# ScalarE normalises all four input tiles, VectorE joins the fourth, and GpSimd makes the factors before its last residual tile

## Chip, cores and metric

The kernel runs on one core of a Trainium2 chip. The metric is the device time of one launch in microseconds; the median of three runs is given.

## The reference, cut to what matters

The input x is (2, 4096, 512) in float32. Two blocks follow one another, each adding to its input.

```python
s  = sigmoid(silu(x @ s_w1.T + s_b1) @ s_w2.T + s_b2)      # x: layernorm of the input
u  = (x @ B_w.T + B_b) * s
h  = h @ A.T + u_t                                        # step by step over 4096 rows
y  = hs @ C_w.T + C_b + x @ D_w.T + D_b
x1 = input + y * sigmoid(x @ g_w.T + g_b)

chosen = argmax(layernorm(x1) @ gate_w.T)                 # one of 8 experts a row
out    = x1 + layernorm(x1) @ expert_w[chosen].T
```

The change touches only the first layernorm of x, the turning of its rows into columns, and the moment at which x1's last quarter is made.

## The kernel before, in words

The 8192 rows go through 16 bodies (b = 0 to 15) of 512 rows: two sequences, 256 rows of each, in four tiles of 128 rows (NT = 4). A body is written out by hand for each engine, as one long list, and the engines meet at semaphores. Every matmul has float32 operands split in a high and a low part, so one product is three matmuls (L1476 to L1478, `mm3`). After the bodies come 71 slots that apply the experts to sorted rows; the change leaves them alone.

What stands in body b on TensorE (L1638): `y_state(b-1)` (four products with the state of the body before), the two `s1` products of all four tiles, the `scan` product, then y and gate products of the four tiles with the steps of the scan strewn in between: `to_pairs`, `to_chunks`, `over(0)` to `over(5)`, `to_middles`, `down`. Each step of the scan is a small matmul (L1620 or L1476), VectorE's sum of its result (L1050, L1052 or L1058), and VectorE's split into high and low: a CAST (L1042) and a subtraction (L1044) that read and write SBUF. The next step on TensorE waits for the split. The first gate product of tile i waits for `gate_sum(b, i-1)` (L1080), which empties the bank.

The input of body b+1 is made during body b, tile by tile:
- SyncE loads it to `xin`; VectorE makes statistics and mean and variance (`ln1_stats`, `ln1_mv`, L992 and L998).
- GpSimd makes the factors `rs1` and `shift1` for four tiles at once (`rstd1`, L573).
- Tiles 0 and 1 are normalised by ScalarE (L756), tiles 2 and 3 by GpSimd (`normalise_late`, L632), which stands behind `rstd1`, the scatter and `add_identity`.
- ScalarE copies the float32 rows as two planes of 16 bits (`halve`, L768), SyncE turns them with a DMA transpose (`flip`, L370), ScalarE joins the planes again (`join`, L795) and makes the high part (`high`, L802), VectorE the low part (`low`, L1249). The first s1 product of the next body needs all four high parts, its last four matmuls (L1665) all four low parts.

GpSimd's list in body b (L635): `residual(b-1)` for four tiles, each two multiplications (L592) and two additions (L596) of 128x256; `rstd1(b+1)`; `scatter(b-2)`, four indirect DMAs (L618); `add_identity` (L627); `normalise_late` twice; `rstd2(b-1)` (L602 and on), which waits for VectorE's `ln2_mv` (L1097). The residual tiles make x1. Tiles 2 and 3 of x1 are turned by DMA as well in bodies 2 to 14: ScalarE `halve_x1` (L731), SyncE (L458), ScalarE `join_x1` (L737).

VectorE's list ends with `h_lo` (L1354, waits for ScalarE's copy L892), `low(b+1, 1)`, `place` (L1132 to L1141), `low_piece` (L1242, expert weights), `low(b+1, 2)`, `ln2_mv`, `gate_sum(b, 3)`; the next body starts with `low(b, 3)` and `y_biased`.

SyncE issues its transposes in the order x1 tile 2, x1 tile 3, input tiles 0, 1, and later 2, 3.

Of the kernel before, what the change touches and what calls it, by code (L numbers as in the profile page):

```python
# [5 lines left out]
def preln_ssm_moe_kernel(nc, x, A, B_w, B_b, C_w, C_b, D_w, D_b, s_w1, s_b1, s_w2, s_b2, g_w, g_b,  # L6
# [27 lines left out]
    NT = TB // P  # L34
# [40 lines left out]
    with ExitStack() as keep:  # L75
# [109 lines left out]
        for name in ("first_half_loaded bias_loaded cols_loaded A_loaded s1_loaded aux_loaded xin_loaded consts_made consts2_made pad_made ident_made "  # L185
                     "bias_sum w_turned w_hi w_lo pow_psum pow_copied pow_hi pow_lo "
                     "gate_stats gate_mean gate_centred stats1 mv1_ready ve1_ready rstd1_ready neg1_ready shift1_ready xn_ready xn_late xT_psum x_halves joined xT_hi xT_lo "
# [168 lines left out]
        def _(sp):  # L356
# [73 lines left out]
            for b in range(NBLK):  # L430
# [24 lines left out]
                if by_dma(b - 1, NT - 1):  # L455
                    for j in range(2):
                        sp.wait_ge(S_["x1_halves"], 2 * (b - 2) + j + 1)
                        sp.dma_start_transpose(x1_flipped[j], x1_halves[j]).then_inc(x1_turned[j], 16)  # L458
                for n in range(NB):
                    if not last:  # L460
                        flip(b + 1, 2 * n)
                        flip(b + 1, 2 * n + 1)
                    if b + 2 < NBLK:
                        load_x(b + 2, n)
                    if n == 0 and b > 1:
                        load_residual(b, b % 2, b // 2)
# [81 lines left out]
        def _(pool):  # L548
# [24 lines left out]
            def rstd1(b):  # L573
                counted_waits(pool, (S_["mv1_ready"], b + 1))
                nc.gpsimd.tensor_scalar(ve1[:], mv1[:, :, 1], EPS, None, ALU.add).then_inc(S_["ve1_ready"], 1)
                pool.wait_ge(S_["ve1_ready"], b + 1)
                if b > 0:
                    pool.wait_ge(S_["xn_ready"], NT + NT // 2 * (b - 1))
                    wait(pool, S_["xn_late"], NT // 2 * (b - 1))
                nc.gpsimd.tensor_tensor(rs1[:], ve1[:], mhalf[:], ALU.pow).then_inc(S_["rstd1_ready"], 1)  # L580
                counted_waits(pool, (S_["shift1_ready"], b))
                nc.gpsimd.tensor_scalar(neg1[:], mv1[:, :, 0], -1.0, None, ALU.mult).then_inc(S_["neg1_ready"], 1)
                counted_waits(pool, (S_["neg1_ready"], b + 1), (S_["rstd1_ready"], b + 1))
                nc.gpsimd.tensor_tensor(shift1[:], neg1[:], rs1[:], ALU.mult).then_inc(S_["shift1_ready"], 1)

            def residual(b, q):
                pool.wait_ge(xres_loaded[q], 16 * NB * (b // 2 + 1))
                for i in range(NT):
# [40 lines left out]
            def normalise_late(b, i):  # L629

                pool.wait_ge(S_["shift1_ready"], b + 1)
                nc.gpsimd.tensor_scalar(xin[:, i, :], xin[:, i, :], rs1[:, i:i + 1], shift1[:, i:i + 1],  # L632
                                        ALU.mult, ALU.add).then_inc(S_["xn_late"], 1)

            def body(b, q):  # L635
                if b > 0:
                    residual(b - 1, 1 - q)
                if b < LASTB:
                    rstd1(b + 1)
                if b >= 2:  # L640
# [4 lines left out]
                if b < LASTB:  # L645
                    normalise_late(b + 1, 2)
                    normalise_late(b + 1, 3)
# [43 lines left out]
        def _(act):  # L691
# [67 lines left out]
            def halve(b, i):  # L759

                n = turn_of(b, i)
                if i < NT // 2:
                    normalise1(b, i)
                    act.wait_ge(S_["xn_ready"], NT + NT // 2 * (b - 1) + i + 1)
                else:
                    act.wait_ge(S_["xn_late"], NT // 2 * (b - 2) + i + 1)
# [38 lines left out]
            def body(b):  # L805
# [42 lines left out]
                if dma:  # L848
                    halve_x1(b - 1, 2)
                    halve_x1(b - 1, 3)  # L850
                if ahead:
                    halve(b + 1, 0)
# [40 lines left out]
                if ahead:  # L893
# [3 lines left out]
                    join(b + 1, 3)  # L897
# [88 lines left out]
        def _(dve):  # L986
# [265 lines left out]

            def body(b, q, turn):
# [104 lines left out]
                if tail:  # L1358
                    place(old, oldq, oldturn)
                    if dma:  # L1360
# [515 lines left out]
```

## Time and profile before

| | before |
|---|---|
| median of 3 runs | 909.34 us (908.67 to 910.84) |
| profiled execution | 911.03 us |
| its span, first to last instruction | 909.2 us |
| TensorE busy (PE) | 890.7 us, 98% |
| VectorE (DVE) | 684.2 us, 75% |
| ScalarE (ACT) | 635.5 us, 70% |
| GpSimd (POOL) | 426.8 us, 47% |
| granted TensorE clock, mean | 0.998 |

The shares are means over the whole span. Bodies 1 to 15 begin at 56.5, 98.1, 138.8, 179.8, ... and 631.2 us, when `y_state` of the body before begins on TensorE; body 7 begins at 302.73 and body 8 at 343.73. The slots follow the last body. The end of a matmul is modelled in the profile; its start is what can be compared.

### The profile page before, as it was taken

The page shows a single profiled execution, that of the slowest core. Times are in us where ns is not written, and L with a number is a line of the kernel's source. Part 1 is how long each engine was busy: PE and PEld are TensorE (multiplying, and loading weights), DVE is VectorE, ACT ScalarE, POOL GpSimd, SP SyncE. Part 2 cuts the span into 40 slices and gives each one's busy share as a digit, 9 for nine tenths or more (in the row PEclk, how much of TensorE's full clock was granted, in tenths as well). Part 3 has the DMA queues.
Part 4 walks back from the last instruction along what each step waited for, and adds up shares of the span by engine and source line. Part 5 has one row for each costly group of instructions (what it writes and reads, how often), then busy time and mean ns, then how long its engine had stood idle before and what let it go on. Part 6 is the DMA issues. An engine that isn't in the chain of part 4 may idle for free. (4 is left out here: it accounts for less than half of the span.)

```text
span 909.2 us, 15716 instructions
## 1 busy us (share of the span) xinstructions
PE 890.7 (98%) x4413; PEld 719.8 (79%) x4414; DVE 684.2 (75%) x1697; ACT 635.5 (70%) x880; POOL 426.8 (47%) x671
## 2 busy tenths in 40 slices
PE   8999999999999999999999999999999999999996
PEld 7778878787887878787787878787878887888884
DVE  6778888888887888888887888888686465555552
ACT  5568697978879687977879687978634445666661
POOL 1134537282735537282836546282624453433442
PEclk9999999999999999999999999999999999999999
DMA  9436495867758486867768495856989979998871
GB/s 319 131 93 148 93 213 140 200 144 193 157 155 209 101 213 137 201 145 189 148 169 206 95 221 128 202 145 161 293 285 401 370 239 252 216 226 220 196 184 49
DMA packets 231050, 172.37 MB, mean 190 GB/s; under 512 B 155701, under 2 KB 189237, under 8 KB 229952
## 3 DMA queue, kind: packets, MB, share of 16 engines
q1 hardware_dynamic: 220032, 137.71, 60.8%
q0 software_dynamic: 10800, 33.70, 11.3%
q8 instruction: 35, 0.57, 0.3%
q14 instruction: 39, 0.32, 0.1%
q10 hardware_dynamic: 144, 0.07, 0.0%
HBM read 81.63 MB, written 54.68 MB: 150 GB/s over the span
## 5 line engine op out<-in xcount | busy, mean ns | idle before, releaser
L1798 PE MATMUL y<-experts,x1T_hi 128*128 x568 | 180.5, 399 | 0.7 <-DVE x1T_lo L1422 0.7
L666 POOL DMA_INDIRECT out<-gate,ids x71 | 72.6, 1023 | 110.3 <-DVE gate L1441 69.0
L602 POOL TENSOR_SCALAR ln_var_eps<-ln_mean_var 128x4 f32<-128x4 f32 x16 | 3.7, 231 | 252.6 <-DVE ln_mean_var L1097 252.5
L1798 PEld LDWEIGHTS y<-experts,x1T_hi 128*128 128x128 f32 x568 | 103.2, 188 | 20.6 <-issue 0.9
L1798 PE MATMUL y<-experts,x1T_lo 128*128 x284 | 111.4, 392 | 0.0
L1476 PE MATMUL gates<-GwT_hi,xT_hi 128*128 128x512 f32 x256 | 105.0, 410 | 1.6
L592 POOL TENSOR_TENSOR y_biased<-y_biased,gate 128x256 f32<-128x256 f32 x120 | 94.1, 805 | 23.8 <-DVE y_biased L1087 23.6
L1476 PE MATMUL y<-DwT_hi,xT_hi 128*128 128x512 f32 x256 | 102.6, 401 | 0.0
L1441 DVE TENSOR_TENSOR gate<-y,raw_weights 128x512 f32<-128x512 f32 x71 | 49.1, 691 | 69.2 <-PE y L1798 65.1
L1478 PE MATMUL gates<-GwT_hi,xT_lo 128*128 128x512 f32 x256 | 100.6, 393 | 0.0
L1477 PE MATMUL gates<-GwT_lo,xT_hi 128*128 128x512 f32 x256 | 100.6, 393 | 0.0
L1478 PE MATMUL y<-DwT_hi,xT_lo 128*128 128x512 f32 x256 | 100.3, 392 | 0.0
L1477 PE MATMUL y<-DwT_lo,xT_hi 128*128 128x512 f32 x256 | 100.2, 392 | 0.0
L596 POOL TENSOR_TENSOR x_rows<-x_rows,y_biased 128x256 f32<-128x256 f32 x120 | 86.7, 743 | 4.7
L795 ACT ACTIVATE joined<-flipped 128x1024 uint16<-128x1024 uint16 x60 | 81.9, 1366 | 8.5 <-DMA flipped<-halves 6.4
L618 POOL DMA_INDIRECT routed_rows<-x_rows,dest x64 | 64.4, 1006 | 24.2 <-issue 23.4
L909 ACT ACTIVATE x1T_hi<-turned 128x512 fp32r<-128x512 f32 x36 | 21.6, 599 | 68.0 <-PE turned L1787 68.0
L768 ACT ACTIVATE halves<-x_in 128x1024 uint16<-128x1024 uint16 x60 | 63.0, 1050 | 1.0
L1798 PEld LDWEIGHTS y<-experts,x1T_lo 128*128 128x128 f32 x284 | 53.3, 188 | 12.0
L1050 DVE TENSOR_TENSOR z<-scan,z 128x126 f32<-128x126 f32 (+6 forms) x128 | 36.0, 281 | 32.2 <-PE scan L1620 30.6
L1476 PEld LDWEIGHTS gates<-GwT_hi,xT_hi 128*128 128x128 f32 x256 | 48.1, 188 | 12.5 <-DVE gate L1080 4.2
L1478 PEld LDWEIGHTS gates<-GwT_hi,xT_lo 128*128 128x128 f32 x256 | 48.1, 188 | 11.1
(285 smaller groups left out, 2335.1 us busy)
## 6 DMA issues: line engine op xcount, KB each, us to landing
raw_weights<-routed_rows SPq DMA_DIRECT2D x71, 258.0 KB, 3.2
x_in<-L_attn_x SPq DMA_DIRECT2D x32, 512.0 KB, 4.5
x_rows<-L_attn_x SPq DMA_DIRECT2D x32, 512.0 KB, 4.9
turned_experts<-raw_weights SPq DMA_DIRECT2D x32, 512.0 KB, 3.5
experts<-turned_experts SPq DMA_DIRECT2D x8, 2048.0 KB, 14.7
raw_weights<-L_ffn_expert_w SPq DMA_DIRECT2D x32, 256.0 KB, 3.1
routed_rows<-padrow SPq DMA_DIRECT2D x9, 258.0 KB
out<-gate,ids POOLq DMA_INDIRECT x71, 4.1
```

Of the source, the lines that this page charges most:

```text
L592: ins = nc.gpsimd.tensor_tensor(yb[:, i, part], yb[:, i, part], gate[:, i, part], ALU.mult)
L596: ins = nc.gpsimd.tensor_tensor(xrow[q][:, i, part], xrow[q][:, i, part], yb[:, i, part], ALU.add)
L618: nc.gpsimd.indirect_dma_start(out=routed, out_offset=bass.IndirectOffsetOnAxis(ap=dest[q][:, i:i + 1], axis=0), in_=xrow[q][:, i, :], in_ ...
L666: nc.gpsimd.indirect_dma_start(out=out_rows, out_offset=bass.IndirectOffsetOnAxis(ap=ids[r][:, 0:1], axis=0), in_=res[r], in_offset=None, ...
L768: nc.scalar.activation(halves[n % 2][:].rearrange("p (h d) -> p h d", h=2), planes(xin[:, i, :]), ACT.Copy).then_inc(S_["x_halves"], 1)
L795: nc.scalar.activation(planes(joined[n % 2][:].rearrange("p k t -> p (k t)")), flipped[n % 2][:].rearrange("p (h k) t -> p h (k t)", h=2), ...
L1050: nc.vector.tensor_tensor(states, both[:, 0], states, ALU.add).then_inc(S_["scan_part"], 1)
L1441: nc.vector.tensor_tensor(res[r], Y[m % 2][:], rows[m][:, 0:D], ALU.add).then_inc(S_["slot_result"], 1)
L1476: nc.tensor.matmul(dst, left[0], right[0], start=first, stop=False)
L1477: nc.tensor.matmul(dst, left[0], right[1], start=False, stop=False)
L1478: return nc.tensor.matmul(dst, left[1], right[0], start=False, stop=last)
L1798: ins = nc.tensor.matmul(Y[m % 2][:], x2T[a][:, k, m % 2 * P:(m % 2 + 1) * P], flat[:, bass.ds(first + (w * KD + k) * D, D)], start=(k == ...
```

## The change

ScalarE normalises all four tiles of the input in `halve`. VectorE gets a function `join` and does the join of tile 3, between `place` and `low_piece`. GpSimd does `rstd1` between residual tile 2 and residual tile 3, and no normalisation. In bodies 2 to 14 ScalarE's `halve(b+1, 0)` stands between `halve_x1` of tiles 2 and 3, and SyncE's transposes follow in the same order. The semaphore `xn_late` is gone, and the counts on `xn_ready` are adapted.

```diff
@@ sync
                         sp.dma_start_transpose(x1_flipped[j], x1_halves[j]).then_inc(x1_turned[j], 16)
+                        if j == 0:
+                            flip(b + 1, 0)
                 for n in range(NB):
                     if not last:
-                        flip(b + 1, 2 * n)
+                        if n > 0 or not by_dma(b - 1, NT - 1):
+                            flip(b + 1, 2 * n)
                         flip(b + 1, 2 * n + 1)
@@ gpsimd
-                if b > 0:
-                    pool.wait_ge(S_["xn_ready"], NT + NT // 2 * (b - 1))
-                    wait(pool, S_["xn_late"], NT // 2 * (b - 1))
+                wait(pool, S_["xn_ready"], NT * b)
...
-            def normalise_late(b, i):
-
-                pool.wait_ge(S_["shift1_ready"], b + 1)
-                nc.gpsimd.tensor_scalar(xin[:, i, :], xin[:, i, :], rs1[:, i:i + 1], shift1[:, i:i + 1],
-                                        ALU.mult, ALU.add).then_inc(S_["xn_late"], 1)
-
             def body(b, q):
                 if b > 0:
-                    residual(b - 1, 1 - q)
+                    residual(b - 1, 1 - q, range(NT - 1))
                 if b < LASTB:
                     rstd1(b + 1)
+                if b > 0:
+                    residual(b - 1, 1 - q, range(NT - 1, NT))
...
-                if b < LASTB:
-                    normalise_late(b + 1, 2)
-                    normalise_late(b + 1, 3)
@@ scalar
             def halve(b, i):
 
+                normalise1(b, i)
                 n = turn_of(b, i)
-                if i < NT // 2:
-                    normalise1(b, i)
-                    act.wait_ge(S_["xn_ready"], NT + NT // 2 * (b - 1) + i + 1)
-                else:
-                    act.wait_ge(S_["xn_late"], NT // 2 * (b - 2) + i + 1)
+                act.wait_ge(S_["xn_ready"], NT * b + i + 1)
...
                 if dma:
                     halve_x1(b - 1, 2)
+                if ahead:
+                    halve(b + 1, 0)
+                if dma:
                     halve_x1(b - 1, 3)
                 if ahead:
-                    halve(b + 1, 0)
                     halve(b + 1, 1)
...
                     high(b + 1, 2)
-                    join(b + 1, 3)
@@ vector
+            def join(b, i):
+
+                n = turn_of(b, i)
+                dve.wait_ge(x_turned[n % 2], 16 * (n // 2 + 1))
+                dve.wait_ge(S_["joined"], n)
+                dve.wait_ge(S_["xT_lo"], NT + n - 1)
+                nc.vector.tensor_copy(planes(joined[n % 2][:].rearrange("p k t -> p (k t)")),
+                                      flipped[n % 2][:].rearrange("p (h k) t -> p h (k t)", h=2)
+                                      ).then_inc(S_["joined"], 1)
...
                 if tail:
                     place(old, oldq, oldturn)
+                if ahead:
+                    join(b + 1, 3)
+                if tail:
                     if dma:
                         low_piece(b, 0)
```

## Rows read from the trace of the kernel before

**Rows 1.** Timeline of TensorE, body 7: start us, us, engine, line, what.

```profile
328.72 0.39 PE L1478 MATMUL y<-DwT_hi,xT_lo 128*128 128x512 f32 x1
...
330.10 0.39 PE L1477 MATMUL gates<-GwT_lo,xT_hi 128*128 128x512 f32 x1
```

**Rows 2.** Timeline of TensorE, the same place in bodies 2 and 14.

```profile
124.07 0.40 PE L1478 MATMUL y<-DwT_hi,xT_lo 128*128 128x512 f32 x1
...
125.17 0.40 PE L1477 MATMUL gates<-GwT_lo,xT_hi 128*128 128x512 f32 x1
...
616.13 0.39 PE L1478 MATMUL y<-DwT_hi,xT_lo 128*128 128x512 f32 x1
...
617.53 0.39 PE L1477 MATMUL gates<-GwT_lo,xT_hi 128*128 128x512 f32 x1
```

**Rows 3.** Timeline of VectorE, body 7, around the split after `over(1)`.

```profile
327.74 0.68 DVE L1042 CAST chunk_ends<-z 128x124 fp32r<-128x124 f32 x1
328.46 0.65 DVE L1044 TENSOR_TENSOR chunk_ends<-z,chunk_ends 128x124 fp32r<-128x124 f32 x1
329.03 0.68 DVE L1080 TENSOR_TENSOR gate<-gates,g_bias 128x512 f32<-128x512 f32 x1
...
330.33 0.23 DVE L1042 CAST chunk_ends<-z 128x120 fp32r<-128x120 f32 x1
330.59 0.29 DVE L1044 TENSOR_TENSOR chunk_ends<-z,chunk_ends 128x120 fp32r<-128x120 f32 x1
```

**Rows 4.** Timeline of GpSimd, body 7 (in brackets: idle before, and what ended it).

```profile
304.42 0.24 POOL L602 TENSOR_SCALAR ln_var_eps<-ln_mean_var 128x4 f32<-128x4 f32 x1 [16.42 <-DVE ln_mean_var L1097]
...
315.37 1.98 POOL L592 TENSOR_TENSOR y_biased<-y_biased,gate 128x256 f32<-128x256 f32 x2
...
318.94 0.23 POOL L575 TENSOR_SCALAR ln_var_eps<-ln_mean_var 128x4 f32<-128x4 f32 x1
...
321.60 1.09 POOL L618 DMA_INDIRECT routed_rows<-x_rows,dest  x1 [0.62 <-issue]
...
327.38 1.59 POOL L632 TENSOR_SCALAR x_in<-x_in,ln_rstd,ln_shift 128x512 f32<-128x512 f32 x2
```

**Rows 5.** Single lines of code, whole run: count, ns minimum/median/maximum, first and last start.

```profile
L756 ACT ACTIVATE x_in<-x_in,ln_shift,ln_rstd x30: 799/809/817, 35.6 to 610.5; 128x512 f32<-128x512 f32 x30
...
L795 ACT ACTIVATE joined<-flipped x60: 1352/1365/1388, 40.7 to 631.2; 128x1024 uint16<-128x1024 uint16 x60
...
L1434 DVE COPY y_biased<-raw_weights x23: 684/695/818, 751.0 to 884.2; 128x1024 uint16<-128x1024 uint16 x23
```

**Rows 6.** Timeline of ScalarE, end of body 6 and body 7.

```profile
297.38 0.54 ACT L745 ACTIVATE scoresT<-scores 16x128 f32<-16x128 f32 x2 [1.47 <-PE scores L1580]
...
300.58 0.43 ACT L892 ACTIVATE hT_hi<-z 128x256 fp32r<-128x256 f32 x1
...
302.84 1.37 ACT L795 ACTIVATE joined<-flipped 128x1024 uint16<-128x1024 uint16 x1
...
328.65 1.36 ACT L737 ACTIVATE y_biased<-y_biased 128x1024 uint16<-128x1024 uint16 x1 [0.59 <-DMA y_biased<-y_biased]
```

**Rows 7.** Timeline of TensorE, body 7: starts that have a margin.

```profile
302.73 0.39 PE L1476 MATMUL y<-CwT_hi,hT_hi 128*128 128x512 f32 x1
...
307.34 1.07 PE L1665 MATMUL turned<-xT_lo,s1T_hi 128*128 128x512 f32 x4
...
320.03 0.29 PE L1476 MATMUL scan<-z_half_hi,A_powers_hi 128*128 128x256 f32 x1
...
322.44 0.28 PE L1620 MATMUL scan<-chunk_ends,A_powers_hi 128*128 128x256 f32 x1
```

**Rows 8.** Timeline of VectorE, body 7: what those starts need.

```profile
304.90 0.69 DVE L1249 TENSOR_TENSOR xT_lo<-joined,xT_hi 128x512 fp32r<-128x512 f32 x1
...
318.01 0.88 DVE L1220 SCALAR_TENSOR_TENSOR z<-scan,B_b_col,select 128x256 f32<-128x256 f32 x2 [1.96 <-ACT select L841]
...
319.45 0.42 DVE L1044 TENSOR_TENSOR z_half_lo<-z,z_half_hi 128x256 fp32r<-128x256 f32 x1
...
321.71 0.29 DVE L1044 TENSOR_TENSOR chunk_ends<-z,chunk_ends 128x128 fp32r<-128x128 f32 x1
```

More of the change, by code:

```diff
@@ L186, in preln_ssm_moe_kernel @@
                      "bias_sum w_turned w_hi w_lo pow_psum pow_copied pow_hi pow_lo "
-                     "gate_stats gate_mean gate_centred stats1 mv1_ready ve1_ready rstd1_ready neg1_ready shift1_ready xn_ready xn_late xT_psum x_halves joined xT_hi xT_lo "
+                     "gate_stats gate_mean gate_centred stats1 mv1_ready ve1_ready rstd1_ready neg1_ready shift1_ready xn_ready xT_psum x_halves joined xT_hi xT_lo "
                      "s1_psum s1_sig silu_ready silu_hi silu_lo bt_psum s2_psum sel_ready "
@@ L584, in rstd1, with residual @@
                 nc.gpsimd.tensor_tensor(shift1[:], neg1[:], rs1[:], ALU.mult).then_inc(S_["shift1_ready"], 1)
-            def residual(b, q):
+            def residual(b, q, tiles):
                 pool.wait_ge(xres_loaded[q], 16 * NB * (b // 2 + 1))
-                for i in range(NT):
+                for i in tiles:
                     pool.wait_ge(S_["gate_ready"], NT * b + i + 1)
```

## The prediction

> **What bounds the kernel now.** Busy shares first: TensorE works in 98% of the span (table above), so what another engine does less of can't shorten the run by itself; what counts is a place where TensorE stands. The ends of matmuls are modelled, so I read starts in its timeline. In the running part of a body they stand 0.23 us apart, for the narrow scan products 0.11. In body 7 (302.73 to 343.73) one place differs: from the last y product at 328.72 to the second gate product at 330.10 pass 1.38 us [rows 1], where 0.23 + 0.11 + 0.11 + 0.23 = 0.68 would do. So 0.70 us is lost around `over(2)` and the first product of gate tile 1. The same two starts are 1.10 us apart in body 2 and 1.40 in body 14 [rows 2]: 0.42 and 0.72 lost. Bodies 3 to 14, twelve of them, are alike, about 0.71 each, so the place is worth 12 x 0.71 + 0.42 = 8.9 us. It is the only loss of size that repeats.
>
> Its cause is on VectorE [rows 3]. The split after `over(1)` is a CAST of 0.68 us and a subtraction of 0.65, where the next pair takes 0.23 and 0.29. So `gate_sum(b, 0)` ends 0.81 us too late, at 329.71, and TensorE's gate product waits for it. Exactly then GpSimd runs its two late normalisations, 327.38 to 328.97 [rows 4]. The two engines hold each other up.
>
> **The change, part by part,** in the times of body 7.
>
> *GpSimd loses the late normalisations.* The split is then done by 328.3 and the gate sum by 328.9, before TensorE can get there (329.17). That saves at most 0.71 us a body, 8.9 in all, if nothing else of GpSimd slides into this spot.
>
> *ScalarE normalises two more tiles and joins one less:* 2 x 0.81 more and 1.37 less [rows 5]. The first lies in front of `scoresT`, where ScalarE idles 1.47 us [rows 6]: free. The second lies ahead of the copies to hT and moves the last of them from 300.58 to 301.42, ending at 301.85 [rows 6]. VectorE's subtraction behind it (0.42 us) ends near 302.35; `y_state` starts at 302.73 [rows 7]. So 0.4 us is left and the cost is nothing; beyond that margin it would be 1:1.
>
> *VectorE joins the fourth tile.* No row has this copy on VectorE. The nearest is its own 128x1024 uint16 copy, 0.695 us; the far end is the 1.365 of ScalarE's join [rows 5]. Below nothing is excluded, it is an added copy. I take 0.69: same engine, same elements. It comes behind `place`, which moves 0.75 later with the hT copies. Its transpose is issued 0.84 later; before, the join at 302.84 found it there without waiting [rows 6], so 0.1 us of waiting at most is new. Then `low_piece`, two `low`, `ln2_mv` and a gate sum are 0.75 + 0.69 = 1.4 us later, and `low(b+1, 3)` ends at 307.0, not 305.6 [rows 8]; its reader starts at 307.34 [rows 7]: 0.3 to spare, cost nothing. With 1.37 for the join it would be 0.35 late in each of twelve bodies, this term's other end, 4 us in all. The rest of the shift goes into VectorE's 1.96 idle us ahead of z [rows 8].
>
> *GpSimd's own order.* Its chain starts from `ln2_mv` [rows 4], so 1.4 us later, at 305.8. Three residual tiles take it to 316.8, and the meeting with `low_piece` (a pair of 1.98 us that takes 1.44 elsewhere, 0.55 more) [rows 4] comes again, now on tile 2: 317.4. `rstd1` runs from 318.94 until 0.62 before the scatter at 321.60 [rows 4], 2.04 us; it now ends near 319.5, earlier than before though it starts from a later chain. ScalarE asks for the factors at 320.4, so the step itself costs nothing and gains nothing. The fourth residual tile then runs from 319.5 to 322.5, not from 315.4 to 318.9. The four scatters move from 321.60 to about 323.1, and `add_identity` behind them to 328.0.
>
> So the tile leaves a stretch in which VectorE read PSUM or ran statistics, and the price of the new place is of the kind of rows 3. VectorE's first split ends at 319.87 and TensorE reads it at 320.03; the second ends at 322.00 and is read at 322.44 [rows 7, 8]. Margins: 0.1 and 0.4. An operation of a split that meets a long GpSimd one waited 0.45 or 0.36 us [rows 3]. On the first split falls `rstd1`, as now, whose small operations don't slow it, and the tile begins about when the split's last operation (319.45) has started: I take 0, and 0.7 as the other end. The second split lies in the tile's additions. One operation hit costs 0, the margin holds it; both cost 0.8 - 0.4 = 0.4. Which it is turns on 0.05 us: I take 0.2.
>
> The scatters and `add_identity` slide towards the old spot at 327.7. Bounds: 0, and 0.45 for one hit by the same rows; with 0.2 us spare between 328.9 and 329.17 I take 0.12.
>
> *SyncE and the fourth tile of x1.* Its row is complete at 322.5 and not 318.9, so it is halved at 322.5 to 323.5, and its transpose comes behind that of the first input tile. Its join began at 328.65, held 0.59 us by the transpose [rows 6]; in the other bodies it began 0.65 earlier. One place later in the queue I give it up to 0.7 more. ScalarE has 1.47 - 0.81 = 0.66 idle left and 0.4 of margin behind that, so mostly nothing comes through; where the scatters hold the queue, 0.5 to 1 in a body. Mean 0.1.
>
> Sum of a body: -0.71 + 0 + 0.2 + 0.12 + 0.1 = -0.29; times 12 is -3.5. Body 2 loses as much as it gains. Bodies 0, 1 and 15 and the slots behind them get nothing. The profiled execution took 911.03 us, 1.8 above its span, and becomes 907.5. It was 1.7 above the median of 909.34, which becomes 905.8, say 906.
>
> **A rule that speaks against the change.** Two operations of 0.77 us cost the split 0.45 and 0.36 [rows 3, 4], so less than their length. The Trainium skill, "SBUF — State Buffer", section "SBUF: two separate sides", says that a VectorE operation in a two-port mode or with two SBUF inputs and a GpSimd operation exclude each other for the whole instruction, whichever starts first. In kind the trace agrees, in size it shows about half. By the rule at full length both operations of the second split could wait 0.74 each, 1.08 behind the margin instead of 0.2, so +0.6 a body and 916: the time of rival 3, which carries this chance too.
>
> **The rivals.**
> 1. *The whole loss goes.* The fourth residual tile and the scatters fall into gaps between VectorE's splits: -8.9 us, 900.4. For it: GpSimd's phases repeat from body to body, so one lucky place is lucky twelve times. Against: the tile covers 319.5 to 322.5 almost without a hole. Chance 0.18.
> 2. *Gain and price cancel.* The second split takes both hits (0.4) and the old spot is refilled (0.3): 909.3, give or take 1.8. Chance 0.17.
> 3. *Slower, by the first split.* If the tile begins by 319.1 instead of 319.5, both operations of the first split are hit (0.8 against a margin of 0.1: 0.7), and the second costs 0.4 too. Or hits last a whole GpSimd operation, which alone comes to the same. A body then has -0.71 + 0.7 + 0.4 + 0.2 = +0.6, twelve +7: 916. It is decided by 0.4 us of GpSimd's chain, a shift of 1.0 instead of 1.4 or no meeting with `low_piece`. For it: that margin on a chain estimated over 14 us. Against: the 1.4 is the sum of two serial operations that nothing hides. Chance 0.15.
> 4. *Slower, by ScalarE.* The x1 transpose lands over 1.0 us late in most bodies; the hT copies, `y_state` and the fourth tile's low half follow: 0.3 to 0.6 on top of a body's forecast, 909.5 to 913. Chance 0.12.
>
> **How the numbers follow.** The forecast has the remaining 0.38. A measurement of this kernel can tell about 0.2%, 1.8 us, from no change. Faster: 0.33 of the forecast's 0.38, all of rival 1, 0.03 of rival 2: 0.54. Same: 0.05, 0.14 and 0.02 of rival 4: 0.21. Slower: 0.15 of rival 3 and 0.10 of rival 4: 0.25. The range goes from rival 1 to the end of rival 4 and leaves out rival 3, 900 to 913.
>
> **What would show it.** Steps right: splits of 0.23 and 0.29 after `over(1)`, and 0.7 us from the last y product to the second gate product there; a VectorE copy of 0.69 us behind `place`; `rstd1` between the third and the fourth residual tile, at 317.4 in body 7's terms. Forecast wrong: a CAST over 0.5 us just before `to_pairs` (rival 3) or before `to_chunks` together with its subtraction (rival 2); ScalarE idle on the transposed x1 and gaps between matmuls at `y_state` or at the first product on xT_lo (rival 4).

## The result, and the profile after

The changed kernel takes 917.61 us (median of 4 runs, 916.37 to 919.95) beside 909.11 (908.67 to 910.84) of the kernel before on the same chip: ratio 1.0093, 95% interval 1.0067 to 1.0118. It is slower by 8.5 us, where 3.3 less was forecast. The profiled execution took 919.95 us and its span is 918.2, against 909.2 before. The granted clock has a mean of 0.997 beside 0.998, so at most 0.9 us of it can be the clock's.

Body 7 now runs from 307.22 to 349.17, 41.95 us where it took 41.00. First TensorE's timeline, at the three places of body 7 where it loses time (start us, us, engine, line, what; in brackets the idle time before and what ended it):

```profile
326.75 0.40 PE L1483 MATMUL gates<-GwT_hi,xT_lo 128*128 128x512 f32 x1
327.23 0.39 PE L1625 MATMUL scan<-chunk_ends,A_powers_hi 128*128 128x256 f32 x1
327.46 0.28 PE L1625 MATMUL scan<-chunk_ends,A_powers_lo 128*128 128x256 f32 x1
...
333.60 0.39 PE L1483 MATMUL y<-DwT_hi,xT_lo 128*128 128x512 f32 x1
...
334.54 0.40 PE L1482 MATMUL gates<-GwT_lo,xT_hi 128*128 128x512 f32 x1
...
347.90 0.40 PE L1483 MATMUL gates<-GwT_hi,xT_lo 128*128 128x512 f32 x1
349.17 0.48 PE L1481 MATMUL y<-CwT_hi,hT_hi 128*128 128x512 f32 x1 [0.87 <-DVE hT_lo L1356]
```

- **The old place** ([rows 1]): 333.60 to 334.54 is 0.94 us, where it was 1.38 and 0.68 is the least. The loss is 0.26 and not 0.70. Over bodies 2 to 14 it is 3.2 us instead of 8.9.
- **The second split** (`to_chunks`): from 326.75 to the first scan product pass 0.48 where 0.23 would do, and to the second 0.23 where 0.11 would do: 0.37 lost, in each of bodies 3 to 14 (0.65 in body 4), 4.8 us in these twelve. Before there was nothing here.
- **`y_state`**, the start of the next body: 1.27 where 0.23 would do. The product waits for the fourth tile's low half, `hT_lo`. Nine of bodies 2 to 14 have such a gap, of 0.36 to 1.24, together 7.0 us; bodies 3, 6, 10 and 11 have none.

VectorE in the same body, and the start of the next:

```profile
308.07 0.76 DVE L1251 COPY joined<-flipped 128x1024 uint16<-128x1024 uint16 x1
...
310.78 0.68 DVE L1241 TENSOR_TENSOR xT_lo<-joined,xT_hi 128x512 fp32r<-128x512 f32 x1
...
325.95 0.35 DVE L1034 CAST chunk_ends<-z 128x128 fp32r<-128x128 f32 x1
326.33 0.84 DVE L1036 TENSOR_TENSOR chunk_ends<-z,chunk_ends 128x128 fp32r<-128x128 f32 x1
...
332.94 0.60 DVE L1036 TENSOR_TENSOR chunk_ends<-z,chunk_ends 128x124 fp32r<-128x124 f32 x1
...
348.60 0.43 DVE L1356 TENSOR_TENSOR hT_lo<-z,hT_hi 128x256 fp32r<-128x256 f32 x1 [1.93 <-ACT hT_hi L885]
```

The new copy of the join lasts 0.76 (0.69 was taken). The subtraction of the second split lasts 0.84 where the one in [rows 8] took 0.29: that is the gap at 327.23. The subtraction after `over(1)` still lasts 0.60. GpSimd beside it:

```profile
310.45 0.23 POOL L603 TENSOR_SCALAR ln_var_eps<-ln_mean_var 128x4 f32<-128x4 f32 x1 [17.50 <-DVE ln_mean_var L1089]
310.76 1.61 POOL L605 TENSOR_TENSOR x_rows<-ln_var_eps,minus_half 128x4 f32<-128x4 f32 x1
...
324.77 1.45 POOL L593 TENSOR_TENSOR y_biased<-y_biased,gate 128x256 f32<-128x256 f32 x2
326.29 1.48 POOL L597 TENSOR_TENSOR x_rows<-x_rows,y_biased 128x256 f32<-128x256 f32 x2
...
332.92 0.94 POOL L628 TENSOR_TENSOR raw_weights<-raw_weights,ident 128x128 f32<-128x128 f32 x2
```

The fourth residual tile (324.77 to 327.77) covers the second split, as forecast; its additions begin at 326.29 and the subtraction at 326.33. `add_identity` at 332.92 meets the subtraction after `over(1)` at 332.94. Counted from the body's start, the chain begins at 3.2 and the first multiplication at 6.0; before it was 1.7 and 3.9 ([rows 4] holds the first of them). `rstd1` stands between the third and the fourth tile (322.53, or 318.0 in the times of body 7 before, where 317.4 was forecast). Then ScalarE, and the transpose that it waits for, from SyncE's own timeline (issue of the fourth x1 tile):

```profile
327.80 1.06 ACT L725 ACTIVATE y_biased<-x_rows 128x1024 uint16<-128x1024 uint16 x1 [1.04 <-POOL x_rows L597]
...
334.31 1.39 ACT L731 ACTIVATE y_biased<-y_biased 128x1024 uint16<-128x1024 uint16 x1 [1.14 <-DMA y_biased<-y_biased]
...
348.15 0.41 ACT L885 ACTIVATE hT_hi<-z 128x256 fp32r<-128x256 f32 x1
```

```profile
328.89 1.40 SPq L458 DMA_TRANSPOSE y_biased<-y_biased  x1
```

`scoresT` has no idle time before it now: the 1.47 us of [rows 6] are used up. They are body 6's; in body 7 of the kernel before, ScalarE idled three times on the same stretch: 0.45 us, the 0.59 of [rows 6] and 0.81:

```profile
325.44 0.55 ACT L745 ACTIVATE scoresT<-scores 16x128 f32<-16x128 f32 x2 [0.45 <-PE scores L1580]
...
338.37 0.55 ACT L745 ACTIVATE scoresT<-scores 16x128 f32<-16x128 f32 x2 [0.81 <-PE scores L1580]
```

That is 1.85 us together. In the changed kernel ScalarE stands 1.04 us until the fourth x1 tile is there and 1.14 until it is transposed, so the last hT copy starts at 40.93 of the body (348.15 - 307.22). Before it was 38.84: 300.58 [rows 6], 2.15 ahead of a body's end [rows 7] that is 40.99 from its start. The views of the waits of the whole run say how often (engine, line, waits for: us in total, times, longest):

```profile
PE y L1481 <- DVE hT_lo L1356: 5.5, 9, 1.1
...
PE scores L1597 <- ACT scoresT L739: 1.2, 3, 0.6
```

```profile
ACT y_biased L725 <- POOL x_rows L597: 13.1, 13, 1.3
...
ACT y_biased L731 <- DMA y_biased<-y_biased: 9.7, 9, 2.3
...
ACT scoresT L739 <- PE scores L1585: 4.5, 2, 3.8
```

```profile
DVE hT_lo L1356 <- ACT hT_hi L885: 18.4, 14, 2.1
```

Before, `scoresT` let ScalarE idle 27.7 us in all, and the transposed x1 tile 0.6 once. Now the waits for the transposed x1 tile and the gaps at `y_state` come in the same nine bodies. In bodies 3, 6 and 11, which have neither, the last hT copy is 0.83 to 0.94 later than before: close to the 0.84 of the forecast, and nothing is lost there.

**The sum of the spans.** From starts of matmuls, body by body: old place -5.7; second split +4.8; `y_state` +7.0; `tail_back` waiting for `scoresT` in bodies 2, 5 and 12, +1.7; first split in bodies 1, 2 and 15 (1.18, 0.33 and 0.77 where 0.28, 0 and 0 were), +2.0; a gap in body 10 that is gone, -0.4. Together +9.4, beside 918.2 - 909.2 = 9.0.

### The profile page after: what moved, and what is told of

It is laid out like the page before. It is cut to its first block and busy times, and to the rows that moved or that the text cites. A ratio compares the mean times of both kernels' runs of the same rounds, so it can differ in the third digit from the quotient of the medians.

```text
span 918.2 us, 15716 instructions
## 1 busy us (share of the span) xinstructions
PE 892.5 (97%) x4413; PEld 719.9 (78%) x4414; DVE 691.0 (75%) x1712; ACT 640.5 (70%) x895; POOL 414.0 (45%) x641
## 5 line engine op out<-in xcount | busy, mean ns | idle before, releaser
L593 POOL TENSOR_TENSOR y_biased<-y_biased,gate 128x256 f32<-128x256 f32 x120 | 87.4, 751 | 23.2 <-DVE y_biased L1079 22.7
L597 POOL TENSOR_TENSOR x_rows<-x_rows,y_biased 128x256 f32<-128x256 f32 x120 | 92.7, 793 | 4.7
L786 ACT ACTIVATE joined<-flipped 128x1024 uint16<-128x1024 uint16 x45 | 61.3, 1363 | 2.6 <-DMA flipped<-halves 2.3
L1483 PEld LDWEIGHTS y<-DwT_hi,xT_lo 128*128 128x128 f32 x256 | 48.1, 188 | 10.5
```

Of the source, the lines that this page charges most:

```text
L593: ins = nc.gpsimd.tensor_tensor(yb[:, i, part], yb[:, i, part], gate[:, i, part], ALU.mult)
L597: ins = nc.gpsimd.tensor_tensor(xrow[q][:, i, part], xrow[q][:, i, part], yb[:, i, part], ALU.add)
L786: nc.scalar.activation(planes(joined[n % 2][:].rearrange("p k t -> p (k t)")), flipped[n % 2][:].rearrange("p (h k) t -> p h (k t)", h=2), ...
L1483: return nc.tensor.matmul(dst, left[1], right[0], start=False, stop=last)
```

## The experiments

Times are medians in us, each beside the kernel before on the same chip. "Before" and "after" in an edit say which kernel it starts from. The theories: **S** says that ScalarE's slack ahead of `scoresT` and the hT copies was spent more than once; **F** that GpSimd's long operations moved onto VectorE's splits.

| kernel | us | before | ratio (95%) |
|---|---|---|---|
| after (all three parts) | 917.61 | 909.11 | 1.0093 (1.0067 to 1.0118) |
| before, join only | 920.37 | 911.05 | 1.0102 (1.0081 to 1.0123) |
| before, normalising only | 911.86 | 911.05 | 1.0011 (0.9999 to 1.0023) |
| before, order only | 929.08 | 911.05 | 1.0188 (1.0168 to 1.0209) |
| after without the order | 918.80 | 910.99 | 1.0085 (1.0064 to 1.0106) |
| after without VectorE's join | 939.09 | 910.12 | 1.0311 (1.0273 to 1.0348) |
| after, GpSimd's order alone undone | 963.23 | 910.99 | 1.0562 (1.0535 to 1.0589) |
| after, tile 3 not normalised | 917.11 | 910.99 | 1.0062 (1.0039 to 1.0085) |
| after, scatters behind x1's transpose | 921.94 | 911.05 | 1.0118 (1.0094 to 1.0142) |
| after, fourth tile's additions wait | 921.21 | 910.12 | 1.0111 (1.0095 to 1.0128) |
| after, x1 tile 3 behind two input tiles | 966.30 | 910.12 | 1.0610 (1.0588 to 1.0631) |
| before, one wait on GpSimd | 904.43 | 910.99 | 0.9920 (0.9896 to 0.9945) |
| the same, repeated | 903.84 | 910.12 | 0.9923 (0.9909 to 0.9937) |

### The parts of the change alone

**The join alone** (from before; `join(b + 1, 3)` leaves ScalarE, VectorE gets the function of the diff):

```diff
@@ scalar
                     high(b + 1, 2)
-                    join(b + 1, 3)
@@ vector
                     place(old, oldq, oldturn)
+                if ahead:
+                    join(b + 1, 3)
+                if tail:
```

> The kernel before; VectorE joins tile 3 between place and low_piece instead of ScalarE, nothing else. Theory chain (whatever makes ln2_mv later moves GpSimd's whole list of the body onto VectorE's splits): ln2_mv is 0.7 us later, the residual additions of the fourth tile reach the split before to_pairs (16.4 to 17.1 of the body) and TensorE stands there 0.3 to 0.7 us in bodies 2 to 14; y_state does not stand: 913 to 918 us. Rival (the join costs nothing by itself, the loss of after is ScalarE's alone): 908 to 911 us.

920.37, the sign as expected and the size beyond it. VectorE's and GpSimd's timelines at the first split of body 7:

```profile
322.16 0.80 DVE L1041 CAST z_half_hi<-z 128x256 fp32r<-128x256 f32 x1
```

```profile
321.37 1.44 POOL L596 TENSOR_TENSOR x_rows<-x_rows,y_biased 128x256 f32<-128x256 f32 x2
```

The first multiplication is at 5.12 of the body (3.92 before), so the fourth tile ends on the first split, and the CAST takes 0.80 instead of 0.29. TensorE's waits:

```profile
PE scan L1488 <- DVE z_half_lo L1043: 7.2, 15, 0.8
```

There is no gap at `y_state` here, and the old place loses as before. Moving the join is harmful by F alone.

**Normalising alone** (from before; ScalarE normalises and joins all four tiles, GpSimd's two late normalisations go):

```diff
@@ gpsimd
-                if b < LASTB:
-                    normalise_late(b + 1, 2)
-                    normalise_late(b + 1, 3)
@@ scalar
+                normalise1(b, i)
                 n = turn_of(b, i)
-                if i < NT // 2:
-                    normalise1(b, i)
...
+                act.wait_ge(S_["xn_ready"], NT * b + i + 1)
```

> The kernel before; ScalarE normalises all four tiles and still joins all four, GpSimd does not normalise, orders as before. Theory ScalarE: 1.6 us more on ScalarE against 0.66 + 0.4 us of slack; hT copies are late, and the join of tile 3 and its high part behind them too, so that the first s1 product stands about 1 us in a body, while over(2) gains 0.6: 913 to 920 us. Rival (ScalarE at 70% busy has room for it): 901 to 904 us.

911.86, no difference that can be told (interval 0.9999 to 1.0023), better than expected. A typical body takes 40.8, so a good part of the old place's 0.7 is got. It is given back at the first product on the new input tile, 0.33 a body, and around `over(2)` in bodies 5, 9 and 14, which are 0.7 to 0.9 longer than their neighbours. So ScalarE's two more tiles cost something even when its slack covers most of them. There is no gap at `y_state`.

**The order alone** (from before; `rstd1` ahead of the fourth residual tile, and the new order of ScalarE's and SyncE's tiles):

```diff
@@ gpsimd
-                    residual(b - 1, 1 - q)
+                    residual(b - 1, 1 - q, range(NT - 1))
                 if b < LASTB:
                     rstd1(b + 1)
+                if b > 0:
+                    residual(b - 1, 1 - q, range(NT - 1, NT))
@@ scalar
                     halve_x1(b - 1, 2)
-                    halve_x1(b - 1, 3)
                 if ahead:
                     halve(b + 1, 0)
+                if dma:
+                    halve_x1(b - 1, 3)
+                if ahead:
```

> The kernel before; rstd1 ahead of the fourth residual tile and the new order of halves and transposes, nothing else. Theory chain: the fourth tile's additions move 2 us later and lie on the split before to_pairs, TensorE stands 0.5 to 0.8 us there; ScalarE waits up to 1 us for x1 tile 3 but has 1.47 us: 913 to 919 us. Rival (the reorder is free, the loss is ScalarE's load): 908 to 911 us.

929.08, slower than either theory allowed. VectorE, then GpSimd, in body 7 (from 310.24):

```profile
327.21 0.85 DVE L1051 TENSOR_TENSOR z_half_lo<-z,z_half_hi 128x256 fp32r<-128x256 f32 x1
...
333.81 1.02 DVE L1049 CAST chunk_ends<-z 128x126 fp32r<-128x126 f32 x1
334.86 0.78 DVE L1051 TENSOR_TENSOR chunk_ends<-z,chunk_ends 128x126 fp32r<-128x126 f32 x1
```

```profile
326.91 1.74 POOL L599 TENSOR_TENSOR x_rows<-x_rows,y_biased 128x256 f32<-128x256 f32 x2
...
333.75 0.88 POOL L630 TENSOR_TENSOR raw_weights<-raw_weights,ident 128x128 f32<-128x128 f32 x2
334.61 1.66 POOL L635 TENSOR_SCALAR x_in<-x_in,ln_rstd,ln_shift 128x512 f32<-128x512 f32 x2
```

The fourth tile's additions lie on the first split, and `add_identity` with the normalisations, 2.5 us without a hole, on the split one earlier than before. A pair of operations that takes 0.5 takes 1.8 there. This is the price of F when the block that VectorE meets is long: 15 waits of 11.4 us in all at that scan, and 7.5 at the first. There is no gap at `y_state`.

**Without the order** (from after; `rstd1` behind all four tiles, ScalarE's and SyncE's old orders):

```diff
@@ gpsimd
-                    residual(b - 1, 1 - q, range(NT - 1))
+                    residual(b - 1, 1 - q, range(NT))
                 if b < LASTB:
                     rstd1(b + 1)
-                if b > 0:
-                    residual(b - 1, 1 - q, range(NT - 1, NT))
```

> The kernel after with GpSimd's rstd1 behind all four residual tiles again and ScalarE's and SyncE's order of before (x1 tile 3 ahead of input tile 0); only 'ScalarE normalises all, VectorE joins tile 3' is left of the change. Theory ScalarE (the loss of after is ScalarE arriving late at the hT copies, for whatever reason): GpSimd's chain still starts some 1.4 to 2 us later in a body, so the factors come at about 20.3 of the body and not 18.3, ScalarE waits 1.5 us or more for them, and y_state still stands 0.5 to 1.2 us in most bodies: 915 to 925 us. Rival (the loss comes from the place of the x1 transpose and the late fourth residual tile alone): the stalls at y_state go, what is left is the gain at over(2): 902 to 906 us.

918.80, in the range of the expectation, but by another sum: that had 0.5 to 1.2 at `y_state`. ScalarE never waits for the transposed x1, and `y_state` loses 0.2 to 0.4 a body, 3.2 us in all. In its place stands the first split, all bodies:

```profile
PE scan L1475 <- DVE z_half_lo L1030: 7.1, 15, 0.6
```

So the new order clears the first split, and costs about as much elsewhere.

**Without VectorE's join** (from after; `join(b + 1, 3)` back on ScalarE behind `high(b + 1, 2)`):

```diff
@@ scalar
                     high(b + 1, 2)
+                    join(b + 1, 3)
@@ vector
-                if ahead:
-                    join(b + 1, 3)
```

> The kernel after, but ScalarE joins tile 3 again and VectorE does not (rstd1's place, the orders and the four normalisations stay). Theory ScalarE: ScalarE, already late in this kernel, gets 1.37 us more ahead of the fourth high part, so the first s1 product stands 0.5 to 1.3 us in most bodies; GpSimd's list starts 0.7 us earlier and its fourth residual tile moves from the second split onto the first: 918 to 926 us. Rival (the join on VectorE is the main cost of the change, as its 9 us alone suggest): 908 to 913 us.

939.09, far above the expectation. The last two residual operations of body 7 (from 313.22) on GpSimd, and the split on VectorE:

```profile
329.23 1.43 POOL L593 TENSOR_TENSOR y_biased<-y_biased,gate 128x256 f32<-128x256 f32 x2
330.74 1.74 POOL L597 TENSOR_TENSOR x_rows<-x_rows,y_biased 128x256 f32<-128x256 f32 x2
```

```profile
331.04 0.84 DVE L1037 TENSOR_TENSOR z_half_lo<-z,z_half_hi 128x256 fp32r<-128x256 f32 x1
```

The fourth tile begins at 16.0 of the body, 1.5 earlier than after the whole change (17.55), and the first split is hit: 0.7 lost there in every body. With it come 0.5 at the first product on the new tile (the join on ScalarE holds `xT_hi` back) and the gaps at `y_state`:

```profile
PE y L1469 <- DVE hT_lo L1347: 9.4, 12, 1.1
```

The parts can't be added. Order and normalising together cost 29.0; the join, which alone costs 9.3, takes about 20 of them away (ratio 1.0311 to 1.0093): its delay puts GpSimd's fourth tile behind the first split, and it takes 1.4 us off ScalarE.

For `y_state` the parts give a clear picture. Normalising alone has no gap there and the order alone has none; both together, without VectorE's join, have one in each of bodies 2 to 14, 0.3 to 1.24 us. ScalarE's slack covers either and not the two.

### ScalarE's slack

**Tile 3 not normalised** (from after):

```diff
-                normalise1(b, i)
+                if i < NT - 1:
+                    normalise1(b, i)
```

> The kernel after without the normalisation of input tile 3 (that tile goes on unnormalised, so its part of the layernorm is left out). Takes 0.84 us from ScalarE just ahead of the hT copies. Theory ScalarE: each stall at y_state shrinks by up to 0.84 us (7.0 us of them in the profile, in nine bodies), about 1.5 to 2 us stay: 911 to 913 us. Rival (the stalls follow the DMA or VectorE's joining and not ScalarE's load): 916 to 918 us.

917.11, runs from 911.52 to 920.31. What was to go went: the gaps at `y_state` fall from 7.0 us to 0.4, `hT_lo` waits 2.7 us instead of 18.4. The time followed only in part: the profiled run took 6.2 us less than that of the changed kernel, but by the ratios (1.0062 and 1.0093) it is 0.3%, 2.8 us, and the two intervals overlap. The median lies in the rival's range, though the rival's reason (stalls that don't follow ScalarE's load) is refuted by the trace. Gaps of 0.3 to 0.6 at the first two splits, and of 0.5 and 0.9 at `over(2)` in two bodies, came in their place. Only one execution was traced; that these gaps make the spread between executions is a guess.

```profile
DVE hT_lo L1358 <- ACT hT_hi L887: 2.7, 4, 1.3
```

**Scatters behind the transpose** (from after; one wait on GpSimd ahead of the scatters):

```diff
                     residual(b - 1, 1 - q, range(NT - 1, NT))
+                if by_dma(b - 1, NT - 1):
+                    pool.wait_ge(x1_turned[1], 16 * (b - 1))
```

> The kernel after with one wait on GpSimd: the scatter begins only when the transpose of x1's tile 3 is down. Theory ScalarE, by the DMA queue: ScalarE's 9.7 us of waiting for that transpose go nearly to zero, all bodies look like bodies 3, 6, 10 and 11 of the profile after (no gap at y_state), some 8 us less, of which later hits of the scatters on splits take a part back: 909 to 914 us. Rival (the transpose is late because it is issued late, not because scatters are in the queue): 916 to 919 us.

921.94, outside both ranges. ScalarE's wait for the transpose is gone from the view, and so are the gaps at `y_state`: the x1 transpose is issued at 326.66 and GpSimd is released by it at 330.87, 4.2 us later, where 328.89 to 334.31 was 5.4. But GpSimd's scatters now run until 335.8 with `add_identity` behind them. GpSimd, VectorE and TensorE in body 7 (from 305.44):

```profile
330.87 1.10 POOL L619 DMA_INDIRECT routed_rows<-x_rows,dest  x1 [5.32 <-DMA y_biased<-y_biased]
...
335.79 0.92 POOL L628 TENSOR_TENSOR raw_weights<-raw_weights,ident 128x128 f32<-128x128 f32 x2
```

```profile
335.11 0.68 DVE L1036 CAST chunk_ends<-z 128x112 fp32r<-128x112 f32 x1
335.82 0.58 DVE L1038 TENSOR_TENSOR chunk_ends<-z,chunk_ends 128x112 fp32r<-128x112 f32 x1
```

```profile
335.45 0.40 PE L1485 MATMUL gates<-GwT_hi,xT_lo 128*128 128x512 f32 x1
336.45 0.36 PE L1627 MATMUL scan<-chunk_ends,A_powers_hi 128*128 128x192 f32 x1 [0.60 <-issue]
```

1.00 us where 0.23 would do: 0.77 lost at a new split, in ten of bodies 2 to 14. At the second split the first scan product comes 0.58 late in eleven of them, where it was about 0.26. The two experiments agree that 0.84 us less work, or no wait for the transpose, is each enough to free `y_state`. Neither shows a faster kernel.

**x1's tile behind two input tiles** (from after; `flip(b + 1, 1)` and `halve(b + 1, 1)` also go ahead of x1's fourth tile):

```diff
@@ sync
                             flip(b + 1, 0)
+                            flip(b + 1, 1)
@@ scalar
                     halve(b + 1, 0)
+                    halve(b + 1, 1)
                 if dma:
                     halve_x1(b - 1, 3)
-                if ahead:
-                    halve(b + 1, 1)
```

> The kernel after, but x1 tile 3 is halved behind both halve(b+1, 0) and halve(b+1, 1), and its transpose follows both. Takes away ScalarE's 1.05 us of idling for the residual tile (0.7 us of lateness in all bodies) and issues the x1 transpose about 0.7 us later. If the idling is what counts: bodies without a late transpose gain 0.4 at most, 913 to 916 us. If the transpose in the queue is what counts: its waits grow from 9.7 to 15 us or more and the gaps at y_state with them, 920 to 928 us.

966.30. The tile's transpose is one place later in the queue, and this wait grows from 9.7 us to:

```profile
ACT y_biased L733 <- DMA y_biased<-y_biased: 57.3, 13, 5.7
```

TensorE then waits 33.2 us for `scoresT`. More than 40 us follow from a place in a queue, which supports S in kind. It is far beyond the 928 expected, to a small part because the clock fell (about 8 us; last section).

**GpSimd's order alone undone** (from after; `rstd1` behind all four residual tiles, ScalarE's and SyncE's new orders kept):

The edit is GpSimd's part of the diff of the kernel without the order, alone.

> The kernel after, but rstd1 behind all four residual tiles; ScalarE's and SyncE's new order stays. Theory ScalarE: input tile 0 now waits for the factors (about 20.3 of the body) and x1 tile 3 is halved behind it, at 22 and not 20.7: y_state stands longer, 919 to 925 us. The stall of 0.37 us at to_chunks goes, because the fourth tile's additions no longer meet that split. Rival (GpSimd's move of rstd1 is what costs): 905 to 911 us.

963.23. ScalarE now stands in its new order, `halve(b+1, 0)` ahead of x1's fourth tile, and waits there for factors that come late. All behind it is late; in the waits of the run:

```profile
ACT x_in L748 <- POOL ln_shift L585: 40.1, 14, 3.1
ACT y_biased L729 <- DMA y_biased<-y_biased: 31.3, 13, 3.0
```

TensorE waits 29.2 us for `scoresT` in 13 bodies, and the clock fell too (last section). The stall at the second split went, as expected, but the first split stands again (5.8 us). The loss is about 40 us more than was expected.

### The fourth tile on the second split

**The additions wait for the split** (from after):

```diff
                     pool.wait_ge(S_["gated"], NT * b + i + 1)
+                    if i == NT - 1:
+                        pool.wait_ge(S_["scan_lo"], NSTEP * (b + 1) + 2)
```

> The kernel after with one wait on GpSimd: the additions of the fourth residual tile wait for the split before to_chunks. Port theory: the 0.37 us that TensorE stands there in bodies 3 to 14 go; ScalarE gets x1's tile 3 some 0.4 us later and its own lateness at y_state grows by up to that in the nine bodies that have it: 914 to 918 us. Rival (the gap at to_chunks has another cause than GpSimd's additions): the gap stays and the time is 918 to 922 us.

921.21: the rival's number, and not its reason, since the gap went. GpSimd, then ScalarE, in body 7:

```profile
326.57 1.44 POOL L599 TENSOR_TENSOR x_rows<-x_rows,y_biased 128x256 f32<-128x256 f32 x2 [0.56 <-DVE chunk_ends L1038]
```

```profile
328.04 1.06 ACT L727 ACTIVATE y_biased<-x_rows 128x1024 uint16<-128x1024 uint16 x1 [1.48 <-POOL x_rows L599]
```

The 0.37 at the second split is gone from every body, and ScalarE gets its row 0.5 us later. All of bodies 2 to 14 show a gap at `y_state`, of 0.59 to 1.24, where nine did. A body loses at least what it gained: a delay of GpSimd's that frees the split comes out of ScalarE's time.

### The kernel before with one wait

**The late normalisations wait for the split that they met** (from before):

```diff
                 if b < LASTB:
+                    pool.wait_ge(S_["scan_lo"], NSTEP * b + 5)
                     normalise_late(b + 1, 2)
```

> The kernel before with one wait added on GpSimd, ahead of the two late normalisations, for VectorE's split after over(1) (scan_lo, NSTEP*b + 5). Nothing else. Theory port: the two normalisations then fall on gate_sum and on sums that read PSUM, the split takes 0.23 + 0.29 us and the 0.71 us of twelve bodies come back: 900 to 902 us. Rival (the normalisations now meet the next split, after over(2), and TensorE stands there instead): 906 to 910 us.

904.43. GpSimd and TensorE in body 7 (from 299.44):

```profile
325.15 1.55 POOL L632 TENSOR_SCALAR x_in<-x_in,ln_rstd,ln_shift 128x512 f32<-128x512 f32 x2 [1.01 <-DVE chunk_ends L1045]
```

```profile
325.46 0.39 PE L1479 MATMUL y<-DwT_hi,xT_lo 128*128 128x512 f32 x1
...
326.15 0.39 PE L1478 MATMUL gates<-GwT_lo,xT_hi 128*128 128x512 f32 x1
```

0.69 us where it was 1.38 and 0.68 is the least. The normalisations begin 1.0 us later, fall beside the gate sum, and no longer hold the split. Eleven of bodies 2 to 14 take 40.43 to 40.55, 0.5 less than before, for one wait and with nothing moved to another engine. That is less than the 0.7 of the expectation: the scan products of the next step come 0.16 late. By its ratio the kernel gains 7.3 us, not 8.5.

> The kernel before with GpSimd's late normalisations waiting for the split after over(1), timed again in five rounds: ratio 0.992 as measured, interval below 0.995.

903.84, ratio 0.9923 (0.9909 to 0.9937). It is 0.8% faster than the kernel before, and the changed kernel is 1.7% slower than it (1.0093 over 0.9923). It beats both.

## Why the prediction was wrong

Forecast: 906 us, -3.5 by twelve bodies. The span grew by 9.0. Per body, mean of bodies 3 to 14:

| term | forecast | measured |
|---|---|---|
| old place, with what slides into it | -0.71 + 0.12 | -0.45 |
| first split | 0 | 0 |
| second split | +0.2 | +0.40 |
| ScalarE and the fourth x1 tile | +0.1 | +0.56 |
| sum | -0.29 | +0.51 |

Twelve bodies gave +6.0 (their periods add to 498.4 instead of 492.4 us), bodies 1, 2 and 15 gave +0.7, +2.3 and +0.9, and the rest of the span -0.9.

1. **The step that failed most is ScalarE's.** I had "0.66 idle left and 0.4 of margin behind that, so mostly nothing comes through". But ScalarE works in order, and what was left had to cover two new waits as well. I wrote that the tile "is halved at 322.5" without asking what ScalarE does until then, and gave the transpose "one place later in the queue" 0.7. In body 7 ScalarE now waits 1.04 for the residual tile and 1.14 for its transpose, 2.18 in place of 1.85, and works 1.62 more: 1.95 of the 2.09 by which the last hT copy is later. The forecast was 0.84, and the margin 0.84 + 0.4 = 1.24: that leaves 0.85 of the 1.04 lost at `y_state`. The kernels without the normalisation of tile 3, or without the wait for the transpose, have next to no such gaps (0.4 us and none): with either taken away, the rest fits. Nor is anything lost at `y_state` in bodies 3, 6, 10 and 11 of the changed kernel, where ScalarE doesn't wait for the transpose.
2. **GpSimd's chain** was to be 1.4 later and is 2.3 (6.2 and 3.9 of the body in most bodies, 6.0 in body 7). The join gives 0.65 of it, where I had 0.69, and the late hT copies 0.95 (the kernel without VectorE's join: 4.87 - 3.92), where I had 0.75. `rstd2`'s operation at L605 gives 0.55, since it now waits for VectorE and lasts 1.61 (the join alone: 5.12 - 3.92 = 1.20, of which 0.55 is this). I had left that one out.
3. **The second split** was taken at 0.2, between 0 and 0.4. Both operations were hit, and unequally: the subtraction is 0.55 longer and the CAST 0.12, 0.67 against 0.44 is 0.23, and the second of the two scan products comes 0.11 late behind the first, which I had not counted. The sum comes to the bound I had kept for both hit.
4. **The old place.** The cause was right: where the normalisations go, or wait, the split is whole. 0.26 stays, since `add_identity` meets the last subtraction (0.60 instead of 0.29). I had 0.12 for that, the bound was 0.45.
5. **The first split** stayed free, as forecast. Rival 3's price is right as well: without VectorE's join the tile begins at 16.0 of the body, ahead of the 16.4 (319.1) named there, and 0.7 is lost in each body. The order alone and the join alone show the same. That was the nearest danger, and the join's delay kept it away.
6. **Bodies 1, 2 and 15** were given nothing. Body 2 pays the full price at `y_state` and `tail_back` (2.0) and gains 0.29; in 1 and 15, where the chain runs otherwise, and by 0.33 in 2, the first split is hit.
7. **The rivals.** The measured 917.61 is near the 916 of rival 3, which is chance: the first split, its whole reason, is free in bodies 3 to 14. This is rival 4's mechanism, with the wait for the residual tile added, at its price (0.56 - 0.1 = 0.46 on top of the forecast, where it had 0.3 to 0.6), together with a dearer second split, a smaller gain and the outer bodies, none of which rival 4 had. I had joined each rival to a forecast that was otherwise right.
8. **The rule on the shared port.** The Trainium skill, "SBUF — State Buffer", section "SBUF: two separate sides", lets a VectorE instruction in a two-port mode, or one with two SBUF inputs, and a GpSimd instruction (for the latter kind one that reads SBUF) exclude each other: whichever starts first has the port for its whole length, and the other blocks. I took that as a price of one whole GpSimd operation, saw 0.45 and 0.36 for operations of 0.77 in [rows 3] and [rows 4], and wrote that the trace shows "about half". That was a misreading. By the rule the latecomer waits for what is left of the other's operation, and the traces agree closely. In body 7 the CAST at 325.95 met a multiplication with 0.27 left and took 0.12 more; the subtraction at 326.33 met an addition with 0.70 left (half of the pair from 326.29) and took 0.55 more; with the join alone, 0.65 was left and 0.51 came on top. In the traces of the fourteen kernels 206 operations of splits began while one of GpSimd's residual operations had more than 0.16 us to go, and each was lengthened by what was left less 0.13 to 0.15. Where GpSimd's next operation follows at once, the wait can run on: 0.79 at the CAST of 1.02 us, with the order alone, beside both operations of `add_identity`. So the price of a meeting follows from the two start times.

Left open: how the loss at `y_state` divides in the whole kernel. Not normalising tile 3 takes it from 7.0 us to 0.4, taking back the order from 7.0 to 3.2; the wait for the residual tile was not taken away by itself. Nor is it known what join and order do without the normalising, which wasn't tried.

## What to carry to other kernels

When a change spends the slack of an engine that works in order, list all that it adds in front of the same deadline (work, waits for another engine, waits for a DMA) and sum them against one margin; two costs that each fit need not fit together. Where two engines hold each other up at one spot, first try to move the less urgent one by a wait on what it collides with. Here a wait of 1.0 us on GpSimd gave 0.8%, while handing its work to ScalarE gave nothing by itself (1.0011) and lost 0.9% with the join and the order. It takes an engine with time behind the spot: after the late normalisations GpSimd idled 16.4 us ([rows 4]), and in the changed kernel two such waits, ahead of the additions and of the scatters, left the kernel no faster (1.0111 and 1.0118 beside 1.0093). And parts of such a change don't add: the join cost 9.3 us alone and saved about 20 beside the other two.

## What the runs showed of the hardware that I had not expected

- **TensorE's clock can turn a stall into a larger loss.** In the kernel with GpSimd's order undone TensorE stands 2 to 3 us ahead of `tail_back` in most bodies, and in bodies 3, 4, 5, 10, 13 and 14 the matmuls that follow start 0.43 us apart rather than 0.23, which is the lower of the two levels (1.2 GHz and not 2.4). The mean granted clock of the run is 0.986. The stall alone does not decide it: 2.76 us in body 2 and 2.62 in body 7 were followed by the full clock, 2.14 in body 4 was not. Stalls of 1.2 us in the changed kernel left its clock at 0.997. In the kernel with GpSimd's order undone the three largest waits come to 42.5 us (29.2 for `scoresT`, 7.5 for `hT_lo`, 5.8 at the first split) of the 52.3 by which its span is longer than 909.2; some 34 starts that come 0.20 late at the lower clock are about 7 more.
- **A tenth of a microsecond decides whether a small GpSimd operation waits.** The power on 128x4 elements (L604 before, L605 after) lasts 1.04 to 1.05 us in all 16 cases before and has a median of 1.61 after. One of VectorE's `low` operations (two inputs in SBUF) runs beside it in both kernels. Before, in body 7, that one starts 0.16 after it (304.90, [rows 8]), now 0.02 after it (310.78 beside 310.76):

```profile
304.74 1.04 POOL L604 TENSOR_TENSOR x_rows<-ln_var_eps,minus_half 128x4 f32<-128x4 f32 x1
```

  In the kernels before and after, and in those with the join alone, normalising alone, without the order and without VectorE's join, it takes 1.60 or 1.61 wherever a `low` operation of an input tile starts up to 0.03 after it, and 1.04 to 1.06 wherever that start is 0.12 or more behind.
- **A kernel can scatter more than its parent.** Tile 3 not normalised spread over 8.8 us in ten runs, where the kernel before spread over 3.9 in thirteen. That near-zero margins are the reason was not tested.
